# Split halves in the cache rows: keys then values, two scatters per tile, and whole-row value transfers, in a fused conditional-mixing, paged-attention and LoRA kernel

## The reference, cut to what matters

```python
x = x + einsum('bct,bcd->bdt', x, w0[subjects])
x = x + einsum('bct,bcd->bdt', x, w1[conditions])
# attention: 8 query heads, 4 key/value heads of 32, blocks of 16 rows, window 128
k_blocks = k_blocks.at[blk, :, off, :].set(k)      # the 32 new rows of each sequence
v_blocks = v_blocks.at[blk, :, off, :].set(v)
scores = where(allowed, q . k_blocks[block_tables], -inf)
x = x + (softmax(scores) . v_blocks[block_tables]) @ Wo.T
x = x + (x @ W.T + adapter(x))
```

## Time and profile before

| what | value |
|---|---|
| median of 3 runs | 496.12 us (494.07 to 496.88) |
| the profiled execution, its own time | 497.69 us |
| its span, first to last instruction | 495.9 us |
| busy: PE, DVE, ACT, POOL | 382.6, 345.0, 266.1, 107.7 us |
| mean granted TensorE clock | 0.904 of full speed |
| moved by DMA | 73.57 MB in 68866 packets |

### The profile page before, as it was taken

How to read it: one execution, slowest core, us unless ns; L and a number is a source line. 1 busy time by engine, 2 the same in 40 slices (tenths; PEclk the granted TensorE clock), 3 DMA queues, 4 the chain that set the end, 5 groups by cost and what they waited for, 6 DMA issues and landing times.

```text
span 495.9 us, 16985 instructions
## 1 busy us (share of the span) xinstructions
PE 382.6 (77%) x6190; PEld 283.8 (57%) x6190; DVE 345.0 (70%) x1017; ACT 266.1 (54%) x977; POOL 107.7 (22%) x178
## 2 busy tenths in 40 slices
PE   1753777888875006969879999999899999987996
PEld 0342534444442004757767777777777777776785
DVE  6994277898889805647656677677777777765782
ACT  3302555666665105545645766666766676654662
POOL 5300043333334620211211221211211221220000
PEclk9855798999999555799989999999999999998999
DMA  3999122222212066788877768867878969875200
GB/s 111 386 399 385 44 79 74 73 78 72 78 55 81 21 140 169 154 163 172 191 191 168 163 169 171 169 153 165 186 173 160 191 173 162 180 188 128 71 24 23
DMA packets 68866, 73.57 MB, mean 148 GB/s; under 512 B 18190, under 2 KB 65326, under 8 KB 66528
## 3 DMA queue, kind: packets, MB, share of 16 engines
q1 hardware_dynamic: 61968, 39.38, 33.9%
q0 software_dynamic: 6864, 33.72, 25.0%
HBM read 70.83 MB, written 26.21 MB: 196 GB/s over the span
## 4 chain that ended last, share of the span: by engine, by line
PE 32%; DMA 18%; ACT 9%; issue 5%; DVE 1%; SPq 1%; ACTq 0%; DVEq 0%; POOLq 0%
PE probT_bank L1123 6%; ACT rope L608 6%; PE out_bank L1147 5%; DMA kvbuf<-new_scratch,winidx 5%; PE score_banks L1084 4%; PE keys_bank L1066 3%; DMA window<-value_scratch 3%; DMA value_scratch<-kvbuf 3%; PE score_banks L1079 3%; ACT window L599 3%; PE out_bank L1134 3%; DMA out<-early 3%; DMA kvbuf<-in_kv,winidx 2%; PE out_bank L1148 2%; PE out_bank L1141 2%
## 5 line engine op out<-in xcount | busy, mean ns | idle before, releaser
L608 ACT ACTIVATE rope<-score_banks,negm 128x176 f32<-128x176 f32 x256 | 102.0, 414 | 4.2 <-DVE negm L886 4.0
L886 DVE TENSOR_REDUCE negm<-score_banks 128x2 f32<-128x352 f32 x128 | 61.0, 518 | 35.1 <-PE score_banks L1084 34.4
L896 DVE TENSOR_SCALAR rope<-rope,rinv 128x176 f32<-128x176 f32 x256 | 69.6, 314 | 4.6
L624 ACT COPY early<-probT_bank 128x128 f32<-128x128 f32 x64 | 17.0, 266 | 88.4 <-PE probT_bank L1123 88.4
L1011 PE MATMUL probT_bank<-wts,x2T 128*128 128x512 f32 x128 | 63.1, 617 | 1.8 <-DVE early L732 1.8
L433 POOL DMA_INDIRECT new_scratch<-stage,rowidx x32 | 36.5, 1142 | 111.9 <-DVE stage L757 107.0
L903 DVE COPY rope<-probT_bank 128x512 f32<-128x512 f32 x64 | 44.3, 692 | 18.6 <-PE probT_bank L1103 14.9
L608 ACT ACTIVATION_READ_ACCUMULATOR rope<-score_banks,negm 128x1 f32 x256 | 54.3, 212 | 0.0
L1123 PE MATMUL probT_bank<-rope,window 128*32 128x64 f32 x2048 | 43.8, 226 | 6.3 <-issue 3.4
L599 ACT COPY window<-keys_bank 128x352 f32<-128x352 f32 x60 | 46.7, 779 | 1.5 <-PE keys_bank L1066 1.5
L1066 PE MATMUL keys_bank<-ident,kvbuf 88*128 88x88 f32 x240 | 32.8, 262 | 16.0 <-ACT window L599 13.9
(11 more groups left out here) (179 smaller groups left out, 705.4 us busy)
## 6 DMA issues: line engine op xcount, KB each, us to landing
value_scratch<-kvbuf SPq DMA_DIRECT2D x16, 704.0 KB
window<-value_scratch SPq DMA_DIRECT2D x16, 512.0 KB, 11.6
work<-in_x SPq DMA_DIRECT2D x16, 256.0 KB, 2.7
new_scratch<-window SPq DMA_DIRECT2D x2, 2048.0 KB, 12.0
out<-early SPq DMA_DIRECT2D x32, 128.0 KB, 5.8
window<-value_scratch SPq DMA_DIRECT2D x32, 96.0 KB, 8.6
new_scratch<-kvbuf SPq DMA_DIRECT2D x1, 2048.0 KB, 14.2
wts<-in_weights SPq DMA_DIRECT2D x1, 1280.0 KB, 8.2
```

What stands on the lines that cost most here:

```text
L608: ins = a.activation(prob[:, par, P_AT[h]:P_AT[h] + KEYS], psS[:, h, 0:KEYS], ACT.Exp, bias=negm[:, par, h:h + 1], accum_out=sums[:, par, ...
L886: v.tensor_reduce(negm[:, par, 2 * half:2 * half + 2], psS[:, 2 * half:2 * half + 2, 0:KEYS], axis=AX_X, op=ALU.max, negate=True).then_inc ...
L896: ins = v.tensor_scalar(prob[:, par, at], prob[:, par, at], rinv[:, par, h:h + 1], None, ALU.mult)
```

## The change

A cache row now holds a block's 16 key rows, then its 16 value rows (8 KB and 8 KB). `new_scratch` has twice as many rows of half the length, and each tile's new rows go in by two scatters of 128 x 512 bytes, the keys (k = 0) and the values (k = 1), each with its own index column; the value index is the key index plus 16. `scat0` and `scat1` count 32 for each tile in place of 16. `values_out` sends the last 8 KB of each of the 88 partitions as one piece, where before it sent 16 pieces of 512 bytes. The transposes of keys read columns at a stride of 128 in place of 256. The diff, whole but for its context lines:

```diff
--- before.py
+++ after.py
@@ -128,7 +128,7 @@
-        d_new = dram("new_scratch", [ENT * BLOCK, 2 * KVH * HD])
+        d_new = dram("new_scratch", [ENT * 2 * BLOCK, KVH * HD])
@@ -149,7 +149,7 @@
-        rowidx = sb("rowidx", [P, TILES], I32)
+        rowidx = sb("rowidx", [P, 2, TILES], I32)
@@ -289,10 +289,9 @@
-        d_new_blocks = d_new.rearrange("(b s t) n -> s b (t n)", s=3, t=BLOCK)
+        d_new_blocks = d_new.rearrange("(b s r) n -> s b (r n)", s=3, r=2 * BLOCK)
-        d_patched = d_new.rearrange("(e t) n -> e (t n)", t=BLOCK)
-        kvflat = kv.rearrange("n t c -> n (t c)")
+        d_patched = d_new.rearrange("(e r) n -> e (r n)", r=2 * BLOCK)
@@ -328,9 +327,8 @@
-                sp.dma_start(d_val[bass.ds(grp, 1)].rearrange("o (r t) n -> (o r) t n", t=BLOCK),
-                             kvbuf[0:GR, par, :].rearrange("p (t k n) -> p k t n", t=BLOCK, k=2)[:, 1]
-                             ).then_inc(s_v_out[par], 16)
+                sp.dma_start(d_val[bass.ds(grp, 1)].rearrange("o (r t) n -> (o r) (t n)", t=BLOCK),
+                             kvbuf[0:GR, par, BLOCK * P:]).then_inc(s_v_out[par], 16)
@@ -408,7 +406,7 @@
-                g.indirect_dma_start(entries[e], None, kvflat,
+                g.indirect_dma_start(entries[e], None, kv,
@@ -430,13 +428,14 @@
-                g.indirect_dma_start(d_new, bass.IndirectOffsetOnAxis(ap=rowidx[:, n:n + 1], axis=0),
-                                     stage[:, j, 256:512], None, bounds_check=ENT * BLOCK - 1, oob_is_err=False
-                                     ).then_inc(s_scat[j], 16)
+                for k in range(2):
+                    g.indirect_dma_start(d_new, bass.IndirectOffsetOnAxis(ap=rowidx[:, k, n:n + 1], axis=0),
+                                         stage[:, j, 256 + P * k:384 + P * k], None, bounds_check=ENT * 2 * BLOCK - 1,
+                                         oob_is_err=False).then_inc(s_scat[j], 16)
-                g.indirect_dma_start(kvbuf[0:GR, par, :], None, kvflat,
+                g.indirect_dma_start(kvbuf[0:GR, par, :], None, kv,
@@ -463,7 +462,7 @@
-                    pool.wait_ge(s["rowidx"], 1)
+                    pool.wait_ge(s["rowidx"], 2)
@@ -477,7 +476,7 @@
-                pool.wait_ge(s_scat[j], 16 * TILES // 2)
+                pool.wait_ge(s_scat[j], 32 * TILES // 2)
@@ -539,7 +538,7 @@
-                wait_from(act, s_scat[j], i * 16)
+                wait_from(act, s_scat[j], i * 32)
@@ -753,7 +752,7 @@
-                wait_from(dve, s_scat[j], i * 16)
+                wait_from(dve, s_scat[j], i * 32)
@@ -813,7 +812,7 @@
-            ch.mark(v.tensor_scalar(T(2), T(10), float(BLOCK), float(SKIP - BLOCK), ALU.mult, ALU.add))
+            ch.mark(v.tensor_scalar(T(2), T(10), float(2 * BLOCK), float(SKIP - 2 * BLOCK), ALU.mult, ALU.add))
@@ -848,7 +847,8 @@
-            v.tensor_copy(rowidx[:], turned_rows).then_inc(s["rowidx"], 1)
+            v.tensor_copy(rowidx[:, 0], turned_rows).then_inc(s["rowidx"], 1)
+            v.tensor_scalar(rowidx[:, 1], turned_rows, float(BLOCK), None, ALU.add).then_inc(s["rowidx"], 1)
@@ -1064,7 +1064,7 @@
-                                       kvbuf[0:GR, par, KV * (4 * u + o):KV * (4 * u + o) + P], ident[0:GR, 0:GR])
+                                       kvbuf[0:GR, par, P * (4 * u + o):P * (4 * u + o) + P], ident[0:GR, 0:GR])
@@ -1180,7 +1180,7 @@
-                    ins = t_.transpose(bank[:, o * GR:(o + 1) * GR], kvbuf[0:GR, 0, KV * (4 * u + o):KV * (4 * u + o) + P],
+                    ins = t_.transpose(bank[:, o * GR:(o + 1) * GR], kvbuf[0:GR, 0, P * (4 * u + o):P * (4 * u + o) + P],
@@ -1220,7 +1220,7 @@
-    kv = _np.concatenate([t(k)[:, heads[k]].transpose(0, 2, 1, 3).reshape(NBLOCKS, BLOCK, KVH * HD) for k in heads], axis=2)
+    kv = _np.concatenate([t(k)[:, heads[k]].transpose(0, 2, 1, 3).reshape(NBLOCKS, -1) for k in heads], axis=1)
```

## The result

The changed kernel takes 536.53 us (median of 4 runs, 532.95 to 543.65) against 495.10 before (4 runs): a ratio of 1.081, 95% interval 1.074 to 1.087. The forecast was 529 us, with a range of 521 to 541. The profiled execution took 536.84 us.

What follows compares the result with a forecast made beforehand. The prediction took a loop of waits through the scatters' landing to bound 75 to 165 us, PE the attention. 497.69 + 37.7 of losses - 3.6 - 1.5 = 530.3, less 1.6 for the median: 529 us, range 521 to 541.

Steps and rivals of the forecast that it cites:

- The loop: 75 to 165 us: scatters, landing, ACT's copy and squares, DVE's sum, `finish`, next scatter; 6.29 us a lap, growing to 8.87.
- The interval that meets the cache gather: From pair 1 to 2, where the scatter is already held up behind the cache gather: 1.3 us lost.
- the last pair: Tile 31's `finish` waits for the landing, the third scatter for DVE's masks, the fourth follows: 2.8 us lost.
- the setup: Before the first scatter: the index column costs DVE one small operation, 0.1 us.
- the laps: Projection stage, 75 to 165 us: two more scatters per lap add 2.58 us, 33.5 us over 13 laps.
- the values: `values_out` in whole rows: each transfer 1.8 us less than 7.43; gains of 3.6 into attention and 1.5 later.
- ACT's wait before the odd L543 about 3.6 us: Sign of being right: ACT's wait before the odd tile's value copy rises from 1.0 to about 3.6 us.
- the chain of transfers: Way into attention, 165 to 221 us: last scatter, patched gather, values out twice, values in; 3.6 us gained.
- the later stall: PE's 3.17 us idle at 449.23 us, behind ACT's wait for a store: 1.5 us gained, between 0 and about 4.7.
- The values gain nothing: Rival: small pieces are as quick, or the cache gather takes the place; 534 us, chance 0.17.
- TensorE's clock falls: Rival: in the longer laps PE's work doubles to 9.4 us, 7 us more in all; 536 us, chance 0.15.
- The second scatters are hidden: Rival: half-size scatters cost POOL no more together, or its idle time takes them; only gains left, 491 us, chance 0.04.

Runs made afterwards that it cites:

- e4: Changed kernel with its 64 scatters reordered, values first, with separate semaphores for keys and values, and value scatters not waiting for `finish`: 494.75 us, ratio 0.995 to the kernel before.
- e7: Changed kernel, scatters in the old order, with four halves of the staging buffer in place of two: 494.33 us, ratio 1.001 to the kernel before.
- e3: Kernel before with its 1-KB scatter issued twice per tile, first into a spare scratch, then the real one: 540.97 us, ratio 1.093.
- e1: Kernel before with each tile's 1-KB scatter cut into two 512-byte scatters, old rows and value pieces kept: 538.56 us, ratio 1.088.
- e2: Changed kernel without the scatter of new value rows, one 512-byte scatter per tile, for timing only: 492.57 us, ratio 0.991 to the kernel before.
- e6: Kernel e4 with values out in 512-byte pieces again, scratch rows at a pitch of 1 KB: 500.17 us, ratio 1.013 to the kernel before.

## Why the prediction was right

**The mechanism.** Each part of it stood the test. The loop was read rightly from the earlier trace rows: opening it by order (e4) or by buffers (e7) takes the loss away, with POOL's work unchanged; POOL's 3.9 us of idle was no reserve. The price of a scatter by number, taken from gathers of other sizes, holds (e3). The interval that meets the cache gather was to pay 1.3 us and paid 1.31 (7.66 to 8.97); the last was to pay nothing and went from 5.58 to 5.57; the last pair was to pay 2.8 and paid 2.9, for the reason given, the mask operations.

**Where the difference lies.** The sum was 530.3 us and the profiled execution took 536.84. Of these 6.5 us the setup has 2.6, the laps 2.4, the values 1.4 and the last pair 0.1, all on the same side. The cause was right; the loss came out a sixth too low, 32.6 us in the sum against 39.2 between the two profiles.

**The laps were put too low** by 0.2 us: 9.07 on the mean against 8.87, so the twelve regular intervals cost 2.74 each, not 2.58 (and that from pair 0 to 1 cost 2.97). Two terms of the lap were off against each other. The fourth scatter takes 1.31 us in ten of the twelve, where the three others take 0.98 to 1.06; I had taken 0.98 or 0.99 for all. And the landing comes 1.31 us after the instruction's end, not 1.45: half the bytes land 0.14 us sooner. With 0.04 for the later start of the fourth, 0.04 + 0.32 - 0.14 is the 0.22 between 6.53 and 6.31. In the two laps whose fourth scatter took 1.10 and 1.11 us the lap was 8.90 and 8.92, in the ten others 9.08 to 9.12. The long fourth is in e1 (six of twelve) and in e3 (eight) too, so neither the rows nor the bytes cause it; why it takes 0.32 us more I didn't find. The sign "ACT's wait before the odd L543 about 3.6 us" was misworked: by the starts in the prediction the even copy moves too, and 2.3 follows; it was 2.66.

**Setup** took 2.7 us more and the step had 0.1 for it. The first scatter stands at 67.25 in e1, 67.27 in e3, 68.30 in e2, 66.58 in e7 and 70.19 in the changed kernel, 67.47 before: these are single traces, and the changed kernel's is the odd one. The delay is there ahead of what the change adds: DVE's cast of the key indices (L850), just before the added operation of 0.18 us, starts at 61.23 us against 58.40. So I take the 2.7 us for scatter between executions, of which that profile had a bad one; what scattered isn't shown.

**The values** are the step that failed. `values_out` lands in 6.99 us, 0.44 less, not 1.8 less: the rates of the queues' mean packet said too much of this transfer. The Trainium skill's figure of 512 bytes for line rate (DMA: Bandwidth & Descriptors, Specifications) is nearer to that: pieces sixteen times as large gained 6%. And on the way into attention I had counted 3.6 us of gain in the chain of transfers and overlooked that the gathers beside it pay: +2.4 us to the keys of group 2, less the 2.08 us of waiting for values that had gone, is +0.3. From there to the end the changed kernel's trace is 6.1 us shorter; less the same 2.08 that is 4.0, where 1.5 stood for the later stall. So the sum of both was 3.7 where 5.1 stood, with its halves wrong in opposite ways, and that it came near is luck: the stretch behind group 2's keys differs by up to 5.6 us between traces with the same pieces, so these 4.0 us aren't shown to be the stall's or the pieces'.

**The rivals.** "The values gain nothing" was right for the way into attention, and for the whole it isn't refuted. "TensorE's clock falls" was right in its event, and its 536 us is the forecast nearest to what was measured, but by coincidence: the lap leaves PE idle over 3 us, and the mean granted clock over the laps was 0.84 (0.95 before):

```profile
75.00:203.00 128.00, 82.17 (x258) 43.19 (x256) 79.72 (x225) 54.03 (x192) 63.68 (x60) 0.84 0.18 54
```

PE was busy 82.17 of 128 us even so, and the laps are accounted for by the train; a slower PE only used up its own idle time. e7, with the same scatters and a lap of 6.08 us, shows the loop and not PE as the bound. "The second scatters are hidden" is what e4 does, by another route than I named.

## What to carry to other kernels

Where no engine is full, find the loop of waits and ask of each added instruction whether it stands in the loop ahead of the one that somebody waits for; an idle engine is no cover for it. If it does stand there, give each kind of transfer its own semaphore and issue first what is waited for soonest, or add a buffer, before giving the idea up: here the same 64 scatters cost 40 us in one order and nothing in another. And a transfer made quicker can delay those beside it, as the gathers here: name the one that is waited for last there before counting a gain.

## What the runs showed of the hardware

- An indirect scatter of 128 rows occupies POOL 0.98 us and 0.30 of gap at 512 and at 1024 bytes a row; its landing follows 1.31 and 1.45 us after the instruction's end. The last of four in a row took 1.31 us in ten of twelve laps, unexplained.
- POOL's scatter that runs into DVE's two mask operations isn't over until they are: it took 5.80 us and 6.26 after, held through the tensor-tensor operation of 4.42 us as well as through the tensor-scalar one of 2.34. In these traces the start decides: before, the scatter that started 0.19 us ahead of the tensor-tensor operation (163.26) took 1.01 us; in e6 one that started 0.19 us behind it (159.67 against 159.48) took 6.73.
- 704 KB from 88 partitions leave in 7.43 us as 1408 pieces and in 6.99 as 88; a cache gather that started 0.9 us after that landing, beside the next such transfer, landed in 8.14 us beside small pieces (e6) and in 9.92 beside whole rows (e4).
